# Router logits from raw rows with centred gate weights, in parts between projections, in a spherical spiking MoE kernel

## The reference, cut to what matters

```python
x = x + _L0_conv_ref(_ln_c(x), ...)          # spherical transform, mixing, back
t = t + _L0_ffn_ref(_ln_t(t))                # opcode arithmetic on each row
x = x + _L1_conv_ref(_ln_c(x), ...)          # spiking attention over 8 time steps
t = t + _L1_ffn_ref(_ln_t(t), Wg, bg, ...)   # experts, the best 2 of 8

def _ln_t(v, eps=1e-05):
    m = jnp.mean(v, axis=-1, keepdims=True)
    s = jnp.var(v, axis=-1, keepdims=True)
    return (v - m) / jnp.sqrt(s + eps)

logits = jnp.einsum('bsd,de->bse', x, Wg) + bg     # in _L1_ffn_ref, x is the normalised row
topk_vals, topk_idx = jax.lax.top_k(logits, K)     # K = 2
```

## Time and profile before

| | |
|---|---|
| median of 3 runs | 1247.43 us (1244.0 to 1249.71) |
| the profiled execution | 1248.21 us, span 1246.2 us |
| granted TensorE clock over the span | 0.872 of full |
| PE / PEld busy | 980.1 us (79%) / 822.9 us (66%) |
| DVE / ACT / POOL busy | 828.8 us (67%) / 625.8 us (50%) / 550.9 us (44%) |
| HBM | 76 GB/s over the span |

### The profile page before, as it was taken

The page is one execution under the profiler, slowest core; times in us unless marked ns, Lnnn a source line. Parts: engine busy times, 40 slices in busy tenths (PEclk is TensorE's granted clock), DMA queues, the critical chain, the costliest instruction groups (busy, mean ns, idle before and its releaser), DMA issues. The chain is left out here.

```text
span 1246.2 us, 23615 instructions
## 1 busy us (share of the span) xinstructions
PE 980.1 (79%) x6627; PEld 822.9 (66%) x6628; DVE 828.8 (67%) x2699; ACT 625.8 (50%) x1334; POOL 550.9 (44%) x707
## 2 busy tenths in 40 slices
PE   9958838767677676876777541499999999999997
PEld 7848825545456464664555530388888888888886
DVE  7724435746759889797885664266666666666665
ACT  3434413475597868778754530244444444444443
POOL 3310001012133566676665764355555554555454
PEclk9979969976778898788877555699999999999999
DMA  8668576900010010000000100111111111111110
GB/s 341 287 186 286 187 212 158 254 19 20 21 51 20 28 46 22 19 26 13 29 15 31 37 25 34 41 51 35 45 48 50 41 48 52 48 41 47 49 40 2
DMA packets 83331, 93.56 MB, mean 75 GB/s; under 512 B 7709, under 2 KB 75549, under 8 KB 79930
## 3 DMA queue, kind: packets, MB, share of 16 engines
q1 hardware_dynamic: 74201, 75.33, 20.5%
q0 software_dynamic: 9056, 17.33, 4.2%
HBM read 56.07 MB, written 38.32 MB: 76 GB/s over the span
## 5 line engine op out<-in xcount | busy, mean ns | idle before, releaser
L1838 POOL DMA_INDIRECT out_dram<-res,index x155 | 154.9, 999 | 216.3 <-DVE res L1904 187.8
L1947 ACT ACTIVATE sil<-ps_h 128x512 f32<-128x512 f32 x155 | 92.6, 597 | 253.0 <-PE ps_h L1999 253.0
L1869 DVE TENSOR_TENSOR act_rows<-ps_h,sil 128x512 f32<-128x512 f32 x155 | 107.2, 692 | 132.3 <-ACT sil L1947 132.3
L2018 PE MATMUL ps_y<-r_raw,aT 128*128 x1240 | 163.8, 275 | 0.0
L159 POOL DMA_INDIRECT slots<-x_sb,r_pos x128 | 129.4, 1011 | 48.3 <-issue 37.3
L2018 PEld LDWEIGHTS ps_y<-r_raw,aT 128*128 128x128 f32 x1240 | 150.7, 192 | 0.1
L1997 PE MATMUL ps_h<-r_raw,uTh 128*128 x310 | 136.6, 441 | 1.6 <-DVE uTl L1863 1.6
L1998 PE MATMUL ps_h<-r_raw,uTh 128*128 x310 | 123.7, 399 | 0.0
L1999 PE MATMUL ps_h<-r_raw,uTl 128*128 x310 | 122.1, 394 | 0.0
L1089 PE MATMUL ps_q<-wqkv,zT 128*128 128x256 f32 x256 | 113.0, 533 | 0.0
L1089 PE MATMUL ps_q<-zT,wqkv 128*128 128x128 f32 x256 | 71.3, 371 | 33.9 <-DVE ps_q L1057 18.3
(11 more groups left out here) (257 smaller groups left out, 2361.9 us busy)
## 6 DMA issues: line engine op xcount, KB each, us to landing
wc<-in_mixing_weights SPq DMA_DIRECT2D x8, 2048.0 KB, 14.8
slots<-zero SPq DMA_DIRECT2D x4, 2652.0 KB, 23.2
pay<-slots SPq DMA_DIRECT2D x39, 272.0 KB, 2.9
x_sb<-in_token_rows SPq DMA_DIRECT2D x8, 1088.0 KB, 6.8
sblk<-coefficients SPq DMA_DIRECT2D x16, 256.0 KB, 6.1
mixed<-mo SPq DMA_DIRECT2D x16, 256.0 KB, 8.2
gin<-mixed SPq DMA_DIRECT2D x16, 256.0 KB, 14.2
r_raw<-in_L_ffn_W SPq DMA_DIRECT2D x8, 508.0 KB
```

Source lines behind the costliest of these rows:

```text
L1838: nc.gpsimd.indirect_dma_start(out_rows, bass.IndirectOffsetOnAxis(at, 0), res[:, m % RES, :], None, bounds_check=TOKENS - 1, oob_is_err=F ...
L1869: nc.vector.tensor_tensor(act_rows[:, k], ps_h[:, k, :, DFF:], sil[:, k], ALU.mult).then_inc(s_act, 1)
L1947: nc.scalar.activation(sil[:, k], ps_h[:, k, :, 0:DFF], ACT.Silu).then_inc(s_sil, 1)
L2018: ins = nc.tensor.matmul(dst, aT[:, k, (2 * e + h) * P:(2 * e + h + 1) * P], raw[:, 4 + h, col], start=(h == 0), stop=(h == 1))
```

## The change

1. `route_rows` and the tile `r_y` go. `route_turn` transposes the raw rows of `x_sb`, and waits for the output added (s_x) in place of the normalised rows.
2. At the start a matmul of (I - 1/C) with `wg` gives `wg_c`, which VectorE copies out of PSUM; the logits use it. `route_choose` first multiplies the logits with the scale of each row, then adds `bg`: one link more in its chain, and a wait for the scale (s_rn).
3. The logits come in four parts of four tiles at rounds 4 to 7, one group is turned in each of the rounds 3 to 6, and, but for the last two blocks, all through the first bank.
4. TensorE gets a function `between`, called ahead of `project`: it holds turn, ranks (at round 1, not 0), route_turn and parts of the logits. They stood in `beside`, behind `project` and `key_values`.
5. On VectorE route_start goes from round 0 to 1, route_turned_over from 1 to 2, route_scale from 2 to 3.
6. ScalarE gets a function `ahead`, called ahead of `sign_projected` from block 1 on: major and route_major, 4 + 4 u rows, 4 + 4 x rows, and z_rows(n, 2) at round 7. The others stay in `behind`.
7. In the tail the calls of route_rows go, the others stay.

```diff
-        CHOOSE_LINKS, START_LINKS, HALF_LINKS, PLACE_LINKS = 15, 11, 13, 19
+        CHOOSE_LINKS, START_LINKS, HALF_LINKS, PLACE_LINKS = 16, 11, 13, 19
...
             dve.wait_ge(s_lg, v + 1)
+            dve.wait_ge(s_rn, v + 1)
...
-            chain.link(nc.vector.tensor_tensor(lg[:, :, :], logits_bank(v).rearrange("p (q e) -> p q e", e=E),
-                                               bg[:, :].unsqueeze(1).broadcast_to([P, NT, E]), ALU.add))
+            by_tile = lambda x: x.rearrange("p (b j) e -> p b j e", j=2)
+            chain.link(nc.vector.tensor_tensor(by_tile(lg[:, :, :]), by_tile(logits_bank(v).rearrange("p (q e) -> p q e", e=E)),
+                                               payload(SCALE, v).unsqueeze(3).broadcast_to([P, B, 2, E]), ALU.mult))
+            chain.link(nc.vector.tensor_tensor(lg[:, :, :], lg[:, :, :], bg[:, :].unsqueeze(1).broadcast_to([P, NT, E]), ALU.add))
...
         def route_turn(pe, v, g):
-            pe.wait_ge(s_ry, v * G + g + 1)
+            pe.wait_ge(s_x, (v + 1) * B)
...
+            elif v < NP2 - 2:
+                pe.wait_ge(s_rz, v * G + g)
...
-                ins = nc.tensor.transpose(route_bank(v, g)[:, q * P:(q + 1) * P], r_y[:, g * G + q, :], ident[:, :])
+                ins = nc.tensor.transpose(route_bank(v, g)[:, q * P:(q + 1) * P], tile(v)(g * G + q), ident[:, :])
...
-        def route_logits(pe, v):
-            pe.wait_ge(s_rz, v * G + 4)
+        def route_logits(pe, v, g0=0, g1=G):
+            pe.wait_ge(s_rz, v * G + g1)
+            if v < NP2 - 2 and g0 == 0:
+                need(pe, s_ranked, v)
+            if v == 0:
+                pe.wait_ge(s_centred, 2)
...
+                nc.vector.tensor_scalar(centre[:, :], ident[:, :], -1.0 / C, None, ALU.add)
...
+                dve.wait_ge(s_centred, 1)
+                nc.vector.tensor_copy(wg_c[:, :], ps_log[:, 0:E]).then_inc(s_centred, 1)
...
-                    if b == 0 and r >= 1:
-                        route_start(dve, r - 1, output_done[r], NT - 2)
+                    if b == 0 and r >= 0:
+                        output_done[r].upto(NT - 2)
+                    if b == 1 and r >= 1:
+                        route_start(dve, r - 1)
                     if b == 1 and r >= 0:
                         route_stats(dve, r, output_done[r])
-                    if b == 1 and r >= 1:
+                    if b == 2 and r >= 1:
                         route_turned_over(dve, r - 1)
-                    if b == 2 and r >= 1:
                         route_place(dve, r - 1)
-                    if b == 2 and r >= 0:
+                    if b == 3 and r >= 0:
                         route_scale(dve, r)
...
+                def ahead(i, b):
+                    n, r = i + 1, i - 2
+                    if b in (0, 1, 2):
+                        major(act, i, b + 1)
+                    if b == 0 and n < NP2:
+                        u_rows(act, n, 0, 4)
+                    if b == 1 and n < NP2:
+                        u_rows(act, n, 10, 14)
+                    if b == 2 and n < NP2:
+                        x_rows(act, n, 4, 8)
+                    if b in (3, 4, 5, 6) and r >= 0:
+                        route_major(act, r, b - 3)
+                    if b == 3 and n < NP2:
+                        x_rows(act, n, 12, NT)
+                    if b == LAST and n < NP2:
+                        z_rows(act, n, 2)
...
+                        if i:
+                            ahead(i, b)
                         sign_projected(act, i, b)
                         if k >= 1:
                             spike_output(act, *divmod(k - 1, B))
+                        if i == 0:
+                            ahead(i, b)
                         behind(i, b)
...
+                nc.tensor.matmul(ps_log[:, 0:E], centre[:, :], wg[:, :], start=True, stop=True).then_inc(s_centred, 1)
                 turn(pe, 0, 0)
...
+                def between(i, b):
+                    r = i - 2
+                    if b == 1 and r >= 1:
+                        route_rank(pe, r - 1)
+                    if b in (0, 1, 2) and i:
+                        turn(pe, i, b + 1)
+                    if b in (4, 5, 6, 7) and r >= 0:
+                        route_logits(pe, r, b - 4, b - 3)
+                    if b in (3, 4, 5, 6) and r >= 0:
+                        route_turn(pe, r, b - 3)
...
+                        between(i, b)
                         project(pe, i, b)
```

More of the change, by code:

```diff
@@ L719, in opcode_and_spikes @@
         r_tmp = sb("r_tmp", [P, 4, NT], at=a)
-        r_y = sb("r_y", [P, NT, C], at=a)
+        centre = sb("centre", [P, P], at=a)
+        wg_c = sb("wg_c", [P, E], at=a)
         lg = sb("lg", [P, NT, E], at=a)
@@ L758, in opcode_and_spikes @@
         s_rn = sem("r_scale_shift")
-        s_ry = sem("r_normalised")
+        s_centred = sem("r_gate_centred")
         s_rt = sem("r_transposed")
@@ L1153, in turn @@
             if g == 0:
-                need(pe, s_rz, (w - 3) * G + 3)
+                need(pe, s_rz, (w - 2) * G)
             for q in range(G):
@@ L1159, in route_bank @@
         def route_bank(v, g):
-            return ps_q[:, g % 2] if v == NP2 - 1 else ps_t[:, g % 2]
+            if v == NP2 - 1:
+                return ps_q[:, g % 2]
+            return ps_t[:, g % 2] if v == NP2 - 2 else ps_t[:, 0]
         def logits_bank(v):
@@ L1179, in route_turn @@
             for q in range(G):
-                ins = nc.tensor.transpose(route_bank(v, g)[:, q * P:(q + 1) * P], r_y[:, g * G + q, :], ident[:, :])
+                ins = nc.tensor.transpose(route_bank(v, g)[:, q * P:(q + 1) * P], tile(v)(g * G + q), ident[:, :])
             ins.then_inc(s_rt, 1)
-        def route_logits(pe, v):
-            pe.wait_ge(s_rz, v * G + 4)
+        def route_logits(pe, v, g0=0, g1=G):
[4 more added lines that the diff above has]
+                pe.wait_ge(s_centred, 2)
             if v == NP2 - 1:
                 pe.wait_ge(s_kvm, NP2 * 4)
-            for q in range(NT):
-                ins = nc.tensor.matmul(logits_bank(v)[:, q * E:(q + 1) * E], rT[:, q, :], wg[:, :], start=True, stop=True)
-            ins.then_inc(s_lg, 1)
+            for q in range(g0 * G, g1 * G):
+                ins = nc.tensor.matmul(logits_bank(v)[:, q * E:(q + 1) * E], rT[:, q, :], wg_c[:, :], start=True, stop=True)
+            if g1 == G:
+                ins.then_inc(s_lg, 1)
         def route_rank(pe, v):
@@ L1342, in major @@
             nc.scalar.activation(zT[:, g * G:(g + 1) * G, :].rearrange("p q k -> p (q k)"), ps_t[:, 0, :], ACT.Copy).then_inc(s_zT, 1)
[L1344 to L1353, removed]
         def route_major(act, v, g):
             act.wait_ge(s_rt, v * G + g + 1)
-            need(act, s_lg, v)
+            if g == 0:
+                need(act, s_lg, v)
             nc.scalar.activation(rT[:, g * G:(g + 1) * G, :].rearrange("p q k -> p (q k)"), route_bank(v, g), ACT.Copy).then_inc(s_rz, 1)
@@ L1600, in _ @@
                     z_rows(act, 0, g)
+                def ahead(i, b):
[14 more added lines that the diff above has]
+                        z_rows(act, n, 2)
                 def behind(i, b):
                     n, r = i + 1, i - 2
-                    if b in (0, 1, 2) and i < NP2:
-                        major(act, i, b + 1)
                     if b == 0 and n < NP2:
-                        u_rows(act, n, 0, 10)
+                        u_rows(act, n, 4, 10)
                     if b == 0 and r >= 1:
@@ L1611, in behind @@
                     if b == 1 and n < NP2:
[L1612 removed]
+                        u_rows(act, n, 14, NT)
                         x_rows(act, n, 0, 4)
                     if b == 2 and n < NP2:
[L1615 to L1628 removed]
+                        x_rows(act, n, 8, 12)
                     if b == 6 and n < NP2:
@@ L1632, in behind @@
                     if b == LAST and n < NP2:
-                        z_rows(act, n, 2)
                         major(act, n, 0)
```

36 lines of the change are left out of this document (3 added, 33 removed).

## The result

| | before | after |
|---|---|---|
| median, us | 1247.5 (20 runs, 1243.3 to 1253.7) | 1255.2 (20 runs, 1250.7 to 1263.9) |
| ratio, 95% interval | | 1.0061 [1.0047, 1.0075] |
| profiled execution: time; span, us | 1248.2; 1246.2 | 1261.5; 1259.4 |

The change costs 0.6%: 7.7 us by the medians. The profiled execution after lies 6 us above its median, so a difference of the two profiles overstates the loss by about as much.

What follows compares the result with a forecast made beforehand. The loop's bound was taken to change by beat: VectorE, ScalarE, or a chain over three engines. Loop +10.2, start +0.3, tail -10.0 gave +0.5 us: 1248, own range 1241 to 1254, whole range 1236 to 1260.

Steps and rivals of the forecast that it cites:

- slower rival: Also the second rival: TensorE falls to half level behind the idle stretch, slowing K0→1 and rounds 3 to 6: 1260, chance 0.28.
- the 56: Loop, blocks 3 to 6: a block time near 56 us would show the forecast right.
- Step 1: ScalarE's 128 normalised-row ACTIVATEs (52.4 us) go; counted at nothing in the loop, where VectorE covers them.
- Step 2: Logits in four parts, rounds 3 to 6: chain 5.8 us at clock 0.83, under VectorE's 6.3; +1 us over the loop.
- The +8 bound: Upper bound on the loop cost of logits in four parts, charged at +1 us; the lower bound was -5.
- Step 3: ScalarE's rows ahead of the sign: K1→2 +1.0, z rows in K6→7 (8.35) +7.4, K7→0 -1.9 us.
- Step 4: Ranks one round later, between project_out and project(1): K0→1 taken as 7.0 us, -3.0 over the loop.
- Step 5: VectorE's route work one round later: K2→3 grows to 7.95 us; +5.7 over the loop with block 7.
- Step 6: Added waits for scale and ranks cost nothing; the centring at the start is taken as 0.3 us.
- Step 7: Tail: without normalised rows the last choice starts 10.6 us earlier; gain 10 us, bounds 6 and 13.5.
- Rival 1: TensorE stays at full level: K0→1 6.1, rounds 3 to 6 on VectorE's floor, shorter tail logits; 1237, chance 0.30.

Runs made afterwards that it cites:

- algebra_only: The kernel before with only the algebra (raw rows turned, centred weights, scale in the choice, no normalised rows) and none of the moves: 1231.1 us, ratio 0.985.
- dve_back: The kernel after with ranks back behind round 0's projections and VectorE's start, turned-over and scale back in rounds 0, 1, 2: 1244.1 us, ratio 0.9962.
- experiment 3: parts_behind: the kernel after with raw-row turns and the four logits parts behind the projections, ScalarE's copies behind the sign: 1245.2 us, ratio 0.9962.
- experiment 9: The kernel after with raw-row turns and logits parts behind the projections, ranks and VectorE's rounds back, z rows still ahead of the sign: 1226.3 us, ratio 0.9824.
- experiment 8: From the kernel after with z rows, parts, ranks and VectorE's rounds undone (1221.3 us), each also undoing: u/x rows ahead 1222.9; z turns ahead 1227.5; four parts 1227.7.
- z_and_parts: The kernel after with the third z rows behind the sign again, and raw-row turns and logits parts behind the projections: 1230.4 us, ratio 0.986.
- filler: The kernel after with 28 unread matrix multiplications behind the projections of rounds 2 and 3 from block 3 on: 1249.5 us, ratio 1.0007.

## Why the prediction was right, and where it was wrong

The time came out 7 us above the forecast of 1248. It lies within the whole range of 1236 to 1260, but 1 us above the forecast's own range of 1241 to 1254, and nearer to the slower rival's 1260. The change cost 0.6%, at the edge of the 0.5% that a measurement can tell. That the sum came so close is in part luck, two errors against each other: the moves cost 24 us where their terms sum to 10.2, and the algebra gave 17 where 9.7 was forecast. Blocks 3 to 6 took 59.9 us in the profiled execution, not the 56 that was named as a sign of being right.

**Step 1** (normalised rows, nothing in the loop): about right. algebra_only's loop is 3.5 us shorter of 412.5.

**Step 2** (logits in four parts, +1) is the step that failed. Turning 7.5 + 1.0 at the half level into 5.8 by a mean clock of 0.83 was wrong in kind: in all of blocks 3 to 7 of after the chain of K3→4 started at the half level, when VectorE's reset came late (attention stood behind 3.5 to 3.7 us of idle TensorE), and a mean over the loop does not say which level a given place in the chain gets. An idle stretch alone does not bring the half level either: in the kernel before, attention in this beat began at the full level in blocks 3, 4 and 6 behind 3.39 us of idle time, and in dve_back at the half level behind 1.4. The +8 bound was 2 short: taking the parts out of the chain gave 10 us [experiment 3]. The second rival named this, with "one in five beats"; K3→4 was 1.4 to 2.1 us longer in each of blocks 3 to 6. The counter-argument that I held against it, a beat with a clock of 0.57 that still ended at 6.30, was a beat with no pieces in its chain: it is parts_behind's 6.25 at 0.50.

**Step 3** (z rows, +5.5 net): mechanism and direct size were right. K6→7 of blocks 1 and 2 was 8.33 and 8.31 for 8.35 forecast, in blocks 3 to 6 K5→6 took its place (both beats together are 14.5 us in after, and 6.2 + 8.35 in parts_behind), and alone it costs 3 to 5 us [experiment 9]. The 1.9 us that K7→0 was to give back came to 0.4. Missed was its effect on the level under the ranks, another 9 us or more. K1→2 at 6.15 for 6.1 held.

**Step 4** (ranks later, K0→1 at 7.0, a gain of 3.0): 7.69, nearly no gain. I had priced 7.4 to 8.5 for the half level and did not choose it. And I missed the turn of z that stood behind them: with the ranks behind the projections and at the full level, moving the turn takes K0→1 from 7.68 to 5.86 [experiment 8]. The level under the ranks counted before too: K0→1 was 7.16 and 7.20 where they took 2.0 us (blocks 4 and 5), 8.35 and 8.93 where they took 3.1 and 3.8 (blocks 3 and 6). Ranks in the chain cost K0→1 nothing while they run at the full level (5.59 in z_and_parts), and the whole gain of the turn at the half level (7.69 after).

**Step 5** (VectorE's load, K2→3 at 7.95): 8.53. The direction and the place were right, the term 0.6 too small; the links of the turned-over half (1.67 after as before) are all there, and a short subtraction grew, see below. Undoing steps 4 and 5 gave 11 us where their terms sum to 2.7.

**Step 6** held: no wait added by the change stands out in the sums of waits of the loop, and the first beat comes at 260.2 us (before 260.4).

**Step 7** (tail, -10.0): 9 less to the last scatter, the last choice 8 nearer to the last attention sign; VectorE's folding of the weights, which ends near 755.7, came behind the logits (747.78 + 5.52 = 753.3), where I had them together.

**Rival 1** (full level) is what filler shows in part: with the clock up, K3→4 is 6.5. It fell because the clock in the loop went down to 0.76, not up. The Trainium skill's TensorE: Matmul & The Clock Gate, in What's actually happening, has throttled as the default that activity releases; the filler agrees, 28 multiplications that nobody reads raised the granted clock of K2→3 from 0.70 to 1.00. Who pays is another question: K3→4 of block 5 in parts_behind ran at 0.50 and lost nothing.

What stays open: what puts a given stretch on the half level, what the ranks and VectorE's rounds are worth apart, how the 10 us of step 2 split between piece and turn, what four parts are worth behind the projections, and why algebra_only's tail gives 3 us more than that of the change (TensorE's level in it is 0.63 for 0.58).

## What to carry to other kernels

Price work that is put into a chain at the level that TensorE may have at that place, not at its mean: here the same chain took 8.0 us mostly at the half level, 6.5 with the clock kept up, and the mean had given 5.8. The same work behind the last instruction that others wait for cost nothing here even at the half level (6.25 us at 0.50). And judge an algebraic gain apart from the reordering that comes with it: here the one was worth 17 us, three of the moves together cost 34, and one move that the forecast gave no credit (turns ahead of the projections) gained 1.8 us in K0→1.

## What the runs showed of the hardware

VectorE's short subtraction in the placing (128x28) takes 188 ns in the median of the kernel before. After, it takes 420 to 630 ns in the five blocks of the loop, each time that it starts beside GpSimd's addition of the output (128x256, 0.67 us), and ends within 0.1 us of it. Block 5, VectorE and GpSimd:

```profile
553.23 0.63 DVE L1029 TENSOR_TENSOR end<-end,opened 128x28 f32<-128x28 f32 x1
```
```profile
553.14 0.67 POOL L1226 TENSOR_TENSOR x_sb<-x_sb,sy 128x256 f32<-128x256 f32 x1 [1.39 <-ACT sy L1397]
```

The three executions of the tail, with no such addition beside them, take 0.19 to 0.22. Over all fourteen traces the subtraction took 423 to 632 ns in the 26 cases in which the addition was already running when it started, and 186 to 221 in the other 86, among them four in which the addition started 0.04 to 0.19 us later. GpSimd's power, which ran beside it in the kernel before, did not slow it. The Trainium skill's Trainium Architecture — The Big Picture, in What this means for kernel authors, says that VectorE and GpSimd contend for one shared pair of ports, by an exclusive lock; these rows agree for the addition and not for the power. No run here shows why the two differ.
